# Two pairs of indirect transfers in flight instead of one, and new orders for all engines

## The reference

```
x = x + 0.5 * ffn(layernorm(x))          # stage A
x = x + attention(layernorm(x))          # stage B
x = x + 0.5 * ffn(layernorm(x))          # stage C, same weights as A

ffn(x):   probs = softmax(x @ gate_w.T + gate_b)            # 8 experts
          vals, idx = top_k(probs, 2)
          expert_e(x) = relu(x @ w1[e] + b1[e]) @ w2[e] + b2[e]   # 128 -> 256 -> 128
          sum of vals * expert_idx(x) over the two chosen experts
attention(x): q = x @ Wq.T; latent = x @ Wkv_down.T (64 wide); k, v from the latent
          8 heads of 32, softmax(q k / sqrt(32)) v, then @ Wo.T
```

## Time and profile before

| | us |
|---|---|
| median of 3 runs | 1338.11 |
| lowest and highest of them | 1331.24, 1339.2 |
| span of the profiled execution | 1336.0 |
| TensorE busy (matmuls) | 1227.4 |
| ScalarE busy | 962.6 |
| VectorE busy | 690.4 |
| GpSimd busy | 470.8 |

### The profile page before, as it was taken

The page is one execution under the profiler, slowest core; times in us unless marked ns, Lnnn a source line. Parts: engine busy times, 40 slices in busy tenths (PEclk is TensorE's granted clock), DMA queues, the critical chain, the costliest instruction groups (busy, mean ns, idle before and its releaser), DMA issues.

```text
span 1336.0 us, 25776 instructions
## 1 busy us (share of the span) xinstructions
PE 1227.4 (92%) x8269; PEld 811.4 (61%) x8269; DVE 690.4 (52%) x2239; ACT 962.6 (72%) x2383; POOL 470.8 (35%) x528
## 2 busy tenths in 40 slices
PE   6989888989999999999999899999799999998795
PEld 2676575576566557666657566667555457665474
DVE  4356446375675446356555365535547546454133
ACT  3338659578788887888887778886778788786331
POOL 2012424434344534234444343433334430243333
PEclk9978999899989998898989989999997879999898
DMA  7305472564645176556445536577421034645672
GB/s 255 141 13 172 145 218 85 175 197 141 190 146 163 48 222 182 160 154 188 132 145 166 150 99 206 166 215 215 147 72 47 31 120 150 195 151 151 206 227 65
DMA packets 159849, 202.04 MB, mean 151 GB/s; under 512 B 16922, under 2 KB 103394, under 8 KB 159715
## 3 DMA queue, kind: packets, MB, share of 16 engines
q1 hardware_dynamic: 144196, 168.90, 41.0%
q0 software_dynamic: 15360, 31.49, 8.1%
q10 hardware_dynamic: 160, 0.01, 0.0%
HBM read 152.49 MB, written 47.84 MB: 150 GB/s over the span
## 4 chain that ended last, share of the span: by engine, by line
DMA 35%; PE 26%; issue 14%; POOL 14%; ACT 7%; DVE 5%; SPq 0%; POOLq 0%; DVEq 0%; ACTq 0%
PE psum L1548 24%; DMA Y<-results_C,posC 10%; DMA slots_C<-xnC,posC 10%; DMA Y<-results_A,posA 8%; POOL Y L1096 7%; DMA slots_A<-xnA,posA 7%; POOL slots_C L1076 4%; ACT psum L1177 2%; POOL slots_A L1076 2%; ACT probs L1168 2%; DVE neg_m L1502 1%; DVE X L1467 1%; ACT xnA L1133 1%; PE psum L1657 1%; PE psum L1625 1%
## 5 line engine op out<-in xcount | busy, mean ns | idle before, releaser
L1548 PE MATMUL psum<-nat 32*128 32x512 f32 x2048 | 413.3, 674 | 17.0 <-ACT psum L1177 8.3
L1502 DVE TENSOR_REDUCE neg_m<-psum 128x1 f32<-128x512 f32 x512 | 318.2, 683 | 202.1 <-PE psum L1548 201.7
L1177 ACT ACTIVATE psum<-psum,neg_m 128x512 f32<-128x512 f32 x512 | 342.8, 692 | 34.5 <-DVE neg_m L1502 33.9
L1168 ACT ACTIVATE probs<-psum 128x512 f32<-128x512 f32 x512 | 267.4, 634 | 45.7 <-PE psum L1548 45.0
L1548 PEld LDWEIGHTS psum<-nat 32*128 32x128 f32 x2048 | 158.5, 193 | 127.0 <-ACT psum L1177 39.2
L1076 POOL DMA_INDIRECT slots_A<-xnA,posA x120 | 117.8, 982 | 255.9 <-DMA slots_A<-xnA,posA 94.6
L1548 PEld LDWEIGHTS psum<-xg_T,wt 128*128 128x128 f32 x1296 | 164.4, 200 | 49.9 <-issue 14.6
L1076 POOL DMA_INDIRECT slots_C<-xnC,posC x120 | 116.4, 970 | 213.0 <-DMA slots_C<-xnC,posC 118.6
L1548 PE MATMUL psum<-xg_T,wt 128*128 128x128 f32 x1296 | 180.9, 290 | 6.6 <-DMA wt<-packed 5.2
L1096 POOL DMA_INDIRECT Y<-results_C,posC x120 | 114.5, 954 | 199.0 <-DMA Y<-results_C,posC 142.0
L1096 POOL DMA_INDIRECT Y<-results_A,posA x120 | 114.8, 957 | 187.7 <-DMA Y<-results_A,posA 128.1
(11 more groups left out here) (188 smaller groups left out, 1383.0 us busy)
## 6 DMA issues: line engine op xcount, KB each, us to landing
wt<-packed SPq DMA_DIRECT2D x324, 320.0 KB, 3.9
xs<-slots_A SPq DMA_DIRECT2D x36, 256.0 KB, 4.2
results_A<-ys SPq DMA_DIRECT2D x36, 256.0 KB
xs<-slots_C SPq DMA_DIRECT2D x36, 256.0 KB, 4.4
results_C<-ys SPq DMA_DIRECT2D x36, 256.0 KB
X<-in_L_attn_x_dram SPq DMA_DIRECT2D x16, 256.0 KB, 6.9
out_dram<-X SPq DMA_DIRECT2D x16, 256.0 KB, 2.5
packed<-probs SPq DMA_DIRECT2D x1, 2560.0 KB, 7.8
```

The costliest lines, as they stand in the source:

```text
L1168: act.activation(probs[:, kt, j, :], at.banks()[j][:], ACT.Exp).then_inc(a_done, 1)
L1177: act.activation(at.banks()[j][:], at.banks()[j][:], ACT.Exp, bias=neg_m[:, g, n, j:j + 1], accum_out=sums[:, g, n, j:j + 1]).then_inc(S[" ...
L1502: V_.tensor_reduce(neg_m[:, g, n, j:j + 1], at.banks()[j][:], AX.X, ALU.max, negate=True).then_inc(S["r_done"], 1)
L1548: return nc.tensor.matmul(dst, w, m, start=start, stop=stop)
```

## The change

GpSimd waits, ahead of a pair, for the landing of the last pair but one (`indirect`, the list of indirect steps alone, against itself shifted by two). Two neighbouring pairs can be in flight at once, so each set of rows has two semaphores, for the tiles with even and with odd number; whoever waits for all four tiles of a batch waits for both. The constants of the planner are all new, `GAP` among them (4.4 to 3.3), and with them the order on every engine and the banks. Durations in `PARTS`, buffers, tiles and chunks stay, and so does everything that is computed.

```diff
@@ -87,17 +87,17 @@
 
 
 
-PERIOD, FIRST_B = 57.89, 143.5
-WANTED = {"norm": -84.66, "scaled": -16.08, "xT": -29.15, ("q", 0): -18.58, ("k", 0): -15.2, ("v", 0): 9.95,
-          ("v", 1): -5.64, ("q", 1): 3.68, ("k", 1): 1.22, "wo": 66.92}
-GROUP_GAP, MAX_PACE, S_FIRST, S_PACE, PV, ADD, SUM = 18.01, 2.93, 22.06, 0.27, -0.13, -1.26, 4.47
-A_LEAD, A_PACE, A_ROUTE, A_NORMS = 40.59, 15.14, 36.72, 8.29
-C_NORM, C_ROUTE, C_FIRST, C_PACE, C_GATHER = 63.2, 31.04, 20.92, 29.32, 52.0
-LOAD_AHEAD, W_AHEAD = -3.49, -1.76
-B_SHIFT = [86.54, -31.84, 6.54, 20.12, -49.35, 18.57, -78.69, -20.22, -54.3, 17.32, 4.45, 0.95, 4.94, -11.17, 16.45, 5.24]
-A_SHIFT = [-41.32, -20.34, -9.8, -16.34, 14.33, 47.38, 30.34]
-C_SHIFT = [10.17, 7.16, -58.43, 37.75, 10.94, -60.54, 5.88]
-GAP = 4.4
+PERIOD, FIRST_B = 62.96, 387.17
+WANTED = {"norm": 190.49, "scaled": 535.73, "xT": -113.75, ("q", 0): -293.31, ("k", 0): -63.09, ("v", 0): 134.62,
+          ("v", 1): 306.98, ("q", 1): -214.01, ("k", 1): -433.94, "wo": 135.24}
+GROUP_GAP, MAX_PACE, S_FIRST, S_PACE, PV, ADD, SUM = 27.18, 6.24, -53.85, 0.88, 1.29, 12.21, 57.07
+A_LEAD, A_PACE, A_ROUTE, A_NORMS = 162.76, 17.36, -78.28, 36.35
+C_NORM, C_ROUTE, C_FIRST, C_PACE, C_GATHER = 70.02, 90.27, 131.38, 35.87, 64.4
+LOAD_AHEAD, W_AHEAD = -121.26, 6.43
+B_SHIFT = [0.76, 228.23, -242.38, -186.44, -527.77, 130.65, -161.27, -166.72, -127.54, -176.06, 99.31, -287.44, 259.55, -270.84, -90.58, 77.56]
+A_SHIFT = [-88.88, -440.61, 24.56, 244.5, 281.84, 233.81, 118.48]
+C_SHIFT = [11.14, 60.23, -119.06, 194.54, -174.03, -86.69, 262.71]
+GAP = 3.3
 
 
 def wanted_attention(b):
@@ -811,8 +811,8 @@
         w_in = [sem(f"w_in{i}") for i in range(4 * W_QUADS)]
         xs_in = [sem(f"xs_in{i}") for i in range(XS_RING)]
         y_out = [sem(f"y_out{i}") for i in range(YS_RING)]
-        gy_in = [sem(f"gy_in{i}") for i in range(Y_RING)]
-        scat_in = {s: [sem(f"scat_in{s}{i}") for i in range(XN_RING)] for s in "AC"}
+        gy_in = [[sem(f"gy_in{i}_{h}") for h in range(2)] for i in range(Y_RING)]
+        scat_in = {s: [[sem(f"scat_in{s}{i}_{h}") for h in range(2)] for i in range(XN_RING)] for s in "AC"}
         zero_in = {s: sem("zero_in" + s) for s in "AC"}
         pack_in = sem("pack_in")
         gate_in = sem("gate_in")
@@ -871,7 +871,7 @@
                     does[step[2]](At(step))
 
         def scattered(s, b):
-            return 32 * TILES * len([old for old in range(b % XN_RING, b + 1, XN_RING) if CHUNK_OF[s][old] != DENSE[s]])
+            return 16 * TILES * len([old for old in range(b % XN_RING, b + 1, XN_RING) if CHUNK_OF[s][old] != DENSE[s]])
 
         def xn_place(s, b):
             return 0 if s == "B" else b % XN_RING * TILES
@@ -955,7 +955,8 @@
                 i = at.turn(quad_turn)
                 if q == 0:
                     for b in range(FIRST[c], FIRST[c] + CHUNKS[c]):
-                        sp.wait_ge(scat_in[s][b % XN_RING], scattered(s, b))
+                        for h in range(2):
+                            sp.wait_ge(scat_in[s][b % XN_RING][h], scattered(s, b))
                 if i >= XS_RING:
                     s0, c0, q0 = quads[i - XS_RING]
                     sp.wait_ge(a_full, counts["a_full", (s0, c0, "xg", q0)])
@@ -1045,7 +1046,8 @@
                 pool.tensor_tensor(pairs[:, kt // 2, j, :], probs[:, kt - 1, j, :], probs[:, kt, j, :],
                                    ALU.add).then_inc(S["p_added"], 1)
 
-            before = {step: old for old, step in zip(order["POOL"], order["POOL"][1:])}
+            indirect = [step for step in order["POOL"] if step[2] in ("scat", "gat")]
+            before = {step: old for old, step in zip(indirect, indirect[2:])}
 
             def apart(at):
 
@@ -1054,10 +1056,10 @@
                 if old and old[2] == "scat":
                     s, c, t = old[0], old[1], old[3]
                     b = FIRST[c] + t // TILES
-                    pool.wait_ge(scat_in[s][b % XN_RING], scattered(s, b) - 32 * (TILES - 1 - t % TILES))
+                    pool.wait_ge(scat_in[s][b % XN_RING][t % 2], scattered(s, b) - 32 * (TILES // 2 - 1 - t % TILES // 2))
                 if old and old[2] == "gat":
                     i = comb_turn[old[:2]]
-                    pool.wait_ge(gy_in[i % Y_RING], ring_count(i, Y_RING, 32 * TILES) - 32 * (TILES - 1 - old[3]))
+                    pool.wait_ge(gy_in[i % Y_RING][old[3] % 2], ring_count(i, Y_RING, 16 * TILES) - 32 * (TILES // 2 - 1 - old[3] // 2))
 
             def scat(at):
 
@@ -1075,7 +1077,7 @@
                 for k in range(2):
                     pool.indirect_dma_start(out=slots[s][:], out_offset=bass.IndirectOffsetOnAxis(ap=pos[s, c % C_RING][:, k, t:t + 1], axis=0),
                                             in_=xn[s][:, xn_place(s, b) + t % TILES, :], in_offset=None).then_inc(
-                        scat_in[s][b % XN_RING], 16)
+                        scat_in[s][b % XN_RING][t % 2], 16)
 
             def gat(at):
 
@@ -1095,7 +1097,7 @@
                 for k in range(2):
                     pool.indirect_dma_start(out=Y[:, i % Y_RING, k, n, :], out_offset=None, in_=results[s, c][:],
                                             in_offset=bass.IndirectOffsetOnAxis(ap=pos[s, c % C_RING][:, k, t:t + 1], axis=0)).then_inc(
-                        gy_in[i % Y_RING], 16)
+                        gy_in[i % Y_RING][n % 2], 16)
 
             walk("POOL", {"add": add, "scat": scat, "gat": gat})
 
@@ -1126,7 +1128,8 @@
                     if CHUNK_OF[s][old] == DENSE[s]:
                         act.wait_ge(a_full, at.count("a_full", "xTf", index=old))
                     else:
-                        act.wait_ge(scat_in[s][old % XN_RING], scattered(s, old))
+                        for h in range(2):
+                            act.wait_ge(scat_in[s][old % XN_RING][h], scattered(s, old))
                 if s == "B":
                     wait(act, d_full, at.count("d_full", "xT", index=b - 1))
                 for n in range(TILES):
@@ -1461,7 +1464,8 @@
                 s, b = at.stage, at.index
                 i = comb_turn[s, b]
                 t = (b - FIRST[CHUNK_OF[s][b]]) * TILES
-                dve.wait_ge(gy_in[i % Y_RING], ring_count(i, Y_RING, 32 * TILES))
+                for h in range(2):
+                    dve.wait_ge(gy_in[i % Y_RING][h], ring_count(i, Y_RING, 16 * TILES))
                 for k in range(2):
                     for n in range(TILES):
                         last = V_.scalar_tensor_tensor(out=X[:, b % X_RING, n, :], in0=Y[:, i % Y_RING, k, n, :],
```

## The result

| | us |
|---|---|
| before, median of 4 runs in the comparison | 1338.65 (1331.24 to 1341.69) |
| after, median of 4 | 1671.11 (1663.73 to 1673.11) |
| ratio, with its 95% interval | 1.2479 (1.2422 to 1.2536) |
| span of the profiled execution after | 1667.6 |

The account below looks back on a forecast made before the run. Two nearly full lines were taken to bound the kernel: TensorE, busy 1227.4 of 1336.0 us, and GpSimd's pairs. 1336.0 - 9 - 12 - 14 = 1301, given as 1303 against the median; range 1264 to 1350.

Parts of the forecast that it names:

- The pairs: GpSimd's 240 gather and scatter pairs: spacing falls from 4.74 to 2.6 us, ends 2.54 and 3.8; their line shrinks 504 us.
- Can the DMA engines take it?: GpSimd's DMA queue uses only 8.1% of 16 engines' span; most of a landing is latency, so two pairs overlap well.
- three terms, 9, 12 and 14: TensorE idle time regained, in us: 9 at the kernel's end, 12 from 1149 to 1284, 14 in the other 698.
- The clock: TensorE's granted clock, mean 0.933: no gain or loss taken, with ends of 38 us gained and 17 us lost.
- The end: Last batch's gathers and combine: they finish sooner, until the dense batch ends last; gain 9 us, range 4.6 to 9.1.
- The new orders and semaphores: All engines' planned orders and some 80 added waits: consumers stand a little late, idle time hides the waits; cost 0.
- Hidden: Rival: TensorE's stalls are its own and gathers were early enough, so only the kernel's end moves; 1329 us, chance 0.19.
- Clock: Rival: freed pairs keep expert work ready all the time, so TensorE's clock loss of 38 goes; 1265 us, chance 0.14.
- Slower by orders that count on a spacing that isn't there: Rival: pairs stay 4.74 us apart against 3.3 planned, a tenth of 346 us exposed on TensorE; 1373 us, chance 0.19.
- A mean clock clearly off 0.93: Sign of a wrong forecast: TensorE's mean clock off 0.93 in either direction, to be read as the clock's doing.
- new long waits of TensorE for xs or Y: Sign of a wrong forecast: TensorE newly waiting long for xs or Y; no size given.
- signs of being right: Pairs 2.54 to 3 us apart, landing waits under 100, TensorE leading the chain, DMA under 15%, last sums close, idle about 75.

## Why the prediction was wrong, step by step

Forecast was 1303 (1264 to 1350); the result is 1671. It lies outside on the slow side. On chips 5 and 7 the same kernel takes 1231 to 1234, outside on the fast side.

**"The pairs": the spacing was right, its cover was not.** The forecast took 2.6 us for a pair with 2.54 as the floor; the timeline shows 1.27 us a transfer, 2.54 a pair. The waits for landings fell from 487.4 to about 23 us, where under 100 was expected. No landing took over 5.3 us by the packets, and scatters took 962 to 1172 ns to issue, as before, so that going by the trace was right there. The prediction had set the 3.1 us of the Trainium skill (SBUF — State Buffer, section "SBUF: two separate sides") against issue times; the Trainium skill gives it there for a whole transfer that takes about 0.62 us alone. No run here shows such a stretch, neither in the issue times nor, at 2.2 us in the median, in the whole transfers. The failed step is the cost that this part of the prediction gave to closer transfers: "Can the DMA engines take it? The GpSimd queue uses 8.1% of 16 engines' span". I asked what the closer transfers do to the DMA engines and to GpSimd, and put what they do to the other four engines at nothing, without a reason. Before, every one of the 240 rows had two transfers, with a wait of 2.50 us behind most of them, so no row of before could show a longer one; the step needed a bound of its own for a density that the trace does not show, and it got none. In its place the runs showed that the other engines starve in rows of more than six. The result's 332 us are 227 of idle TensorE and 105 of longer busy time at the lower clock; on chip 2, 284 of 301 us went when the rows were broken. Why it happens on some chips only stays open.

**The forecast on the kind of chip where nothing starves.** The waits alone (old orders, chip 5) cut TensorE's idle time from 108.6 to 1284.4 - 1208.5 = 75.9 us. The forecast expected about 75: its three terms, 9, 12 and 14, are right as a sum for this kernel, which has the orders of before and not the forecast's. At the end the last combine is over 2.2 us after the dense sum (1281.72 and 1279.50) where it was 9.1, so 6.9 of the 9 came; the other two were not compared one by one. What it missed is 19 us of busy time, 1227.4 to 1208.5: the clock rose from 0.933 to 0.944, 144 us at 1.2 GHz instead of 179, worth half of the 35. With the new orders too (chip 7) idle is 68.2 and busy 1156.9, 70.5 less, at 0.964: 2 x 0.036 x 1225.1 = 88 us at 1.2 GHz where it was 179, worth half of the 91, 45 us. The rest of the 70.5 is not explained by the clock's mean. **The clock** was taken at 0 with 38 as its end; on chip 7 its 45 is more than the 40 us of idle time that went, so the term that the sum left out is the largest there.

**"The end"** came as forecast. VectorE's last rows on chip 7:

```profile
1219.10 2.30 DVE L1471 SCALAR_TENSOR_TENSOR X<-Y,gateC,X 128x128 f32<-128x128 f32 x8
1221.32 1.12 DVE L1429 SCALAR_TENSOR_TENSOR X<-psum,givenC,X 128x128 f32<-128x128 f32 x4
```

The last combine is over before the dense batch's last sum, 1221.32 + 1.12, and 2.7 us later the span ends. In the earlier trace rows it was the other way round by 9.1 us. It is so in the result as well.

**"The new orders and semaphores"**, put at 0 in the sum, was wrong by much. On chip 5 the orders cost 131 us with the old waits and win 49 with the new ones (1283.5 to 1234.0). I had compared 2.6 with the planned 3.3 and called it a little late for consumers. That an order made for close pairs packs all steps closer would explain both, but no run changed one constant by itself.

**The rivals.** Hidden (1329): false on either kind. Clock (1265): the higher clock is what chips 5 and 7 show, and more of it; that it comes of expert work being ready, as this rival had it, no run shows. Slower by orders that count on a spacing that isn't there (1373, decided above 3.3 us): its mechanism is real, as the kernel with the old wait shows. I put a tenth of 346 us as exposed; on chip 5 it is 131, 0.38. In the result it did not act, since the spacing was 2.54, and on chip 2 old and new orders are about equally slow: slow by another mechanism than the one that I had priced.

**What was to show it.** "A mean clock clearly off 0.93" was there, 0.834, and I had called that the clock's doing and not the pairs'; it was the pairs', since with broken rows chip 2 goes from 0.850 back to 0.924. The "new long waits of TensorE for xs or Y" were not: the 140.9 us name nothing that is waited for. Most signs of being right were there in a kernel that is a quarter slower: pairs 2.54 us apart, 23 us of waits, TensorE first in the chain with DMA at 1%, both last sums close together. Only the idle time of TensorE, 335 for about 75, and the clock spoke against it: the others watched the pairs, and the pairs were fine.

## What to carry to other kernels

When a wait between two transfers of GpSimd goes, count how many will now follow each other without a pause, and ask what the other engines do meanwhile; a trace in which every row had two says nothing about rows of twenty. Break such rows (here at six transfers: 1637 to 1353 us on one chip, one run, and at no cost that could be measured with the old orders on another), and measure on several chips before believing a gain or a loss: the same program gave 0.92 and 1.22 of the same baseline. Plan orders and waits together, since here each half alone misled about the whole.

For use where the chip can't be chosen, the kernel before is the safe one, at 1331 to 1350 us on all six that were tried (five, if the chip of the result is chip 2); on a chip where nothing starves the changed kernel is the best of all that ran. The old orders with a rest at every third pair (0.9624 on chip 15) might be both, but that kernel did not run on a slow chip.

## What the runs showed of the hardware

- Two kinds of behaviour of one program, by chip or by job. With rows of up to 26 to 40 indirect transfers 1.27 us apart, TensorE is over 0.9 busy up to the 12th on chips 5 and 7, and falls to 0.60 by the 7th and 8th and to 0.09 by the 18th on the chip of the result, and to about a third on chip 2. The kernel before, with rows of two, tells no difference between them.
- In starved stretches instructions that wait for no semaphore stand too: up to 1.76 us idle between matmuls, 48 of SyncE's steps over 0.5 us long. ScalarE, which waits for others, stands for 27.71 us, while DMA's own packets move on (share 0.53 and 152 GB/s from 495 to 502.6 us).
- In traces of the slow kind landing marks are missing: 8405 of some 16,200 are left in the result. They are missing also where nothing starves, from 88 to 99 us and in the kernel with the rest (9242 left at 1353 us). A page that prints "another core or an unknown queue" or "remote" for one core shows this. A blank landing time alone does not: the page of before has two, and there all 7680 of GpSimd's marks are recorded.
- After TensorE's busy share has fallen from 0.77 to 0.15 its granted clock stands at 0.50, where it was 1.00 (487 to 510 us), so in the result starvation is paid twice: 227 us more idle and 105 us more busy.
